# Splitting the last chunk of a graph attention kernel into two softmax units of four groups, with older groups added up two per slot

## What is computed

```python
f = (x @ W_ni.T)[src] + (x @ W_nj.T)[dst] + e @ W_fij.T
f = leaky_relu(f, 0.2)
score = f @ attn
a = softmax of score over the edges of each dst
h = x @ W_node.T
h_out = segment_sum(h[src] * a[:, None], dst)
```

## Time and profile before

| | |
|---|---|
| median of 3 runs | 2160.43 us (2159.26 to 2163.89) |
| the profiled execution's own time | 2163.74 us |
| its span | 2162.0 us |
| mean granted TensorE clock | 0.92 |
| busy share PE, POOL, DVE, ACT | 87%, 74%, 63%, 31% |

### The profile page before, as it was taken

One profiled execution on the slowest core, in us unless ns is written; L12 is line 12 of the kernel. 1 busy time (PEld: TensorE's weight loads), 2 busy tenths in 40 slices (PEclk: granted clock), 3 DMA queues, 4 the chain that ended last, 5 costly groups with the idle time before them and its releaser, 6 DMA issues.

```text
span 2162.0 us, 41030 instructions
## 1 busy us (share of the span) xinstructions
PE 1872.9 (87%) x10816; PEld 1284.3 (59%) x10816; DVE 1351.5 (63%) x4574; ACT 672.6 (31%) x1260; POOL 1593.5 (74%) x1664
## 2 busy tenths in 40 slices
PE   5799999898888899898978998888888888888887
PEld 4366766566565666566756666565555555565656
DVE  6477776665665666665745756656556556555655
ACT  2555444443433434443211112222222222122221
POOL 7777777777777777777577777777777777777771
PEclk9899999989999989988989989989999999989998
DMA  9888898888888888888756776666766766766761
GB/s 321 261 269 287 281 290 268 255 259 253 262 256 254 262 247 266 261 252 252 228 163 181 216 203 199 207 198 195 207 191 201 204 197 197 205 190 199 204 195 41
DMA packets 352481, 490.63 MB, mean 227 GB/s; under 512 B 115219, under 2 KB 217924, under 8 KB 352092
## 3 DMA queue, kind: packets, MB, share of 16 engines
q1 hardware_dynamic: 236803, 249.78, 38.0%
q0 software_dynamic: 78416, 212.69, 33.4%
q10 hardware_dynamic: 37017, 25.40, 3.9%
HBM read 409.00 MB, written 81.38 MB: 227 GB/s over the span
## 4 chain that ended last, share of the span: by engine, by line
PE 41%; DMA 23%; issue 12%; POOL 9%; DVE 7%; ACTq 6%; ACT 2%; POOLq 0%; DVEq 0%; SPq 0%
DMA xsrc<-h_table,idx_slot 11%; PE bSC L935 9%; DMA xsrc<-x_table,idx_slot 9%; POOL xsrc L612 9%; PE pair L946 9%; PE pair L894 8%; PE pair L915 7%; ACTq L778 4%; PE pair L919 3%; ACTq L774 2%; DVE fT L1419 1%; DMA proj<-xsrc 1%; ACT zc L738 1%; PE bX L1000 1%; DVE amat L1267 1%
## 5 line engine op out<-in xcount | busy, mean ns | idle before, releaser
L612 POOL DMA_INDIRECT xsrc<-h_table,idx_slot x804 | 777.1, 967 | 246.9 <-issue 201.3
L612 POOL DMA_INDIRECT xsrc<-x_table,idx_slot x767 | 730.8, 953 | 233.8 <-issue 194.2
L738 ACT ACTIVATE zc<-pair 128x512 f32<-128x512 f32 x416 | 248.4, 597 | 1334.4 <-PE pair L919 1137.7
L1419 DVE TENSOR_TENSOR fT<-pair,zc 128x512 f32<-128x512 f32 x416 | 286.1, 688 | 350.9 <-ACT zc L738 348.1
L894 PE MATMUL pair<-edge_in,wts 128*128 128x512 f32 x832 | 488.3, 670 | 10.3 <-DMA window<-proj 10.3
L915 PEld LDWEIGHTS pair<-ident,xsrc 128*128 128x128 f32 x1600 | 204.8, 152 | 472.1 <-DMA xsrc<-h_table,idx_slot 213.6
L935 PE MATMUL bSC<-fT,attn_at 128*32 128x128 f32 x3328 | 478.9, 291 | 3.7 <-DVE fT L1419 3.7
L946 PEld LDWEIGHTS pair<-amat,xsrc 128*128 128x128 f32 x3328 | 432.8, 201 | 64.1 <-issue 50.6
L946 PE MATMUL pair<-amat,xsrc 128*128 128x42 f32 x3328 | 465.2, 293 | 2.2 <-DVE amat L1269 2.0
L915 PE MATMUL pair<-ident,xsrc 128*128 128x128 f32 x1600 | 275.1, 299 | 191.7 <-DMA xsrc<-h_table,idx_slot 119.5
L935 PEld LDWEIGHTS bSC<-fT,attn_at 128*32 128x32 f32 x3328 | 350.2, 116 | 113.9 <-issue 92.0
(11 more groups left out here) (169 smaller groups left out, 1407.5 us busy)
## 6 DMA issues: line engine op xcount, KB each, us to landing
edge_in<-eT SPq DMA_DIRECT2D x208, 256.0 KB
rel_bc<-relrow_g SPq DMA_DIRECT2D x416, 128.0 KB
h1T<-h SPq DMA_DIRECT2D x208, 256.0 KB
edge_in<-h1T SPq DMA_DIRECT2D x208, 256.0 KB
stage<-h_table ACTq DMA_DIRECT2D x896, 1.0 KB
window<-proj SPq DMA_DIRECT2D x416, 32.0 KB
xsrc<-h_table,idx_slot POOLq DMA_INDIRECT x824, 3.7
xsrc<-x_table,idx_slot POOLq DMA_INDIRECT x767
```

What stands on the lines that cost most here:

```text
L612: pool.indirect_dma_start(xsrc[b][:, i, 0:width], None, table, bass.IndirectOffsetOnAxis(ap=idx_slot[b][:, i:i + 1], axis=0)).then_inc(L.g ...
L738: nc.scalar.mul(zc[s][:, :], bZ[s][:, :], SLOPE).then_inc(L.z_scaled, 1)
L1419: v.tensor_tensor(fT[s][:, :], bZ[s][:, :], zc[s][:, :], ALU.max).then_inc(L.f_made, 1)
```

## The change

The last chunk becomes two units: unit 25 is groups 200 to 203, unit 26 is groups 204 to 207 (16 rows of scores each). Unit 25's softmax steps lie in slots 204 to 208, unit 26's in slots 208 to 212. Slot 208 still adds up group 195; slots 209 to 212 add up two groups each (196 and 197, ..., 202 and 203), and slots 213 to 216 one each (204 to 207). The program ends in slot 217. Slab 24 is summed in slot 212. `dst_rows` is loaded twice in the last chunk, at its slots 2 and 6, behind the `row_maxima` of units 24 and 25; `masks` run in its slots 3 and 7. `FILL` has fewer idle matmuls. Unit 25 has its own weight tiles (`relc_next`, `wcol_next`). Cut to its core:

```diff
-FILL = {0: 1, 1: 2, 2: 5, 3: 3, 4: 2, 5: 1}
+FILL = {0: 1, 1: 1, 2: 2, 3: 1, 4: 2, 5: 1}
+HALF = 4
+def soft_steps(c, g):
+    if not isinstance(c, int):
+        return {g: c - 1} if g <= 4 else {}
+    slot = c * GC + g
+    return {slot - closed(u): u for u in range(CH + 1) if 0 <= slot - closed(u) <= 4}
+def summed(c, g):
+    if not isinstance(c, int):
+        return [c * GC + (g - LAG)]
+    slot = c * GC + g
+    if slot <= NG:
+        return [slot - LAG] if slot >= LAG else []
+    first = NG - LAG + 2 * (slot - NG) - 1
+    if first < NG - HALF:
+        return [first, first + 1]
+    n = slot - (LAG - HALF)
+    return [n] if n < NG else []
...
-                        if g == GC - 2:
-                            if isinstance(c, int) and c == 0:
+                        if g == GC - 2 or (isinstance(c, int) and c == CH - 1 and g == GC - HALF - 2):
+                            u = CH if isinstance(c, int) and c == CH - 1 and g == GC - 2 else c
+                            if isinstance(u, int) and u == 0:
...
-                                sp.wait_ge(L.soft_dve, (c - 1) * 6 + 1)
+                                sp.wait_ge(L.soft_dve, (u - 1) * 6 + 1)
...
+                        for m in sums[1:]:
+                            partial(m // GC, m % GC, m // GC % XB)
...
+                        if static:
+                            past, coming = summed(c, g - 1), summed(c, g + 1)
+                            for m in past[0:1]:
+                                finish(m)
+                            for m in coming[0:1]:
+                                weighted_onehot(m, m % GC, True)
...
+                        if static and c == CH - 1:
+                            if g == GC - HALF - 1:
+                                masks(CH - 1)
+                            if g == GC - 1:
+                                masks(CH)
+                        elif front and g == 6:
                             masks(c)
+                        if static:
+                            for m in past[1:]:
+                                finish(m)
+                            for m in coming[1:]:
+                                weighted_onehot(m, m % GC, True)
```

More of the change, by code:

```diff
@@ L143, in slab_at, with unit_of, first_group, closed @@
     return k * (2 * NB) - LEAD, NB
+def unit_of(n):
+    return CH if n >= NG - HALF else n // GC
+def first_group(u):
+    return NG - HALF if isinstance(u, int) and u == CH else u * GC
+def closed(u):
+    return NG - HALF if isinstance(u, int) and u == CH - 1 else NG if isinstance(u, int) and u == CH else u * GC + GC
+def height(u):
+    return HALF * TG if isinstance(u, int) and u >= CH - 1 else TC
+def soft_steps(c, g):
[14 more added lines that the diff above has]
+    return [n] if n < NG else []
+def slab_steps(n, c, g):
+    if isinstance(c, int):
+        slot = c * GC + g
+        late = (CH + 1) * GC
+        if n == 2 and late - GC <= slot <= late - GC + 4:
+            steps = {late - GC + i: {name: CH - 3} for i, name in enumerate(("rest", "std", "shift", "out", "store"))}
+            steps[late - GC + 4].update(sum=CH - 2, h=CH - 2)
+            return steps[slot]
+        if slot >= late - GC + 4:
+            names = {late - 4: ("sum", "h"), late - 3: ("rows",), late - 2: ("copies", "rest") if n == 1 else ("rest",),
+                     late - 1: ("middle", "low") if n == 1 else ("std", "shift"),
+                     late: ("store",) if n == 1 else ("out", "store")}.get(slot, ())
+            return {name: CH - 2 for name in names}
+    plan = {}
+    if not (isinstance(c, int) and not 2 <= c <= CH - 1):
+        plan.update({6: {"sum": c - 2, "h": c - 2}, 7: {"rows": c - 2}}.get(g, {}))
+    if not (isinstance(c, int) and c < 3):
+        at = ({0: ("copies", "rest"), 1: ("middle", "low"), 2: ("store",)} if n == 1 else
+              {0: ("rest",), 3: ("std",), 4: ("shift",), 5: ("out",), 6: ("store",)})
+        plan.update({name: c - 3 for name in at.get(g, ())})
+    return plan
 def above(eng, sem, value):
@@ L740, in slot @@
                         one_hot(c, g + 1)
[L741 to L747, removed]
[L748 to L753 removed]
+                    steps = soft_steps(c, g)
+                    if 0 in steps:
+                        u, rows = steps[0], height(steps[0])
+                        act.wait_ge(L.score_made, closed(u))
+                        above(act, L.soft_dve, u * 6 - 3)
+                        nc.scalar.copy(score_sb[0:rows, :], bSC[0:rows, 0:P]).then_inc(L.score_copied, 1)
+                    if 2 in steps:
+                        u, rows = steps[2], height(steps[2])
+                        act.wait_ge(L.soft_dve, u * 6 + 3)
+                        nc.scalar.activation(aexp[0:rows, :], seg[0:rows, :], ACT.Exp)
+                        nc.scalar.activation(ecar[0:1, 1:2], ecar[0:1, 0:1], ACT.Exp).then_inc(L.soft_act, 1)
+                    if narrow:
+                        plan = slab_steps(L.n, c, g)
+                        for name, body in (("copies", slab_copies), ("middle", slab_middle), ("std", slab_std),
+                                           ("out", slab_out), ("store", slab_store)):
+                            if name in plan:
+                                body(L, plan[name])
                     if L.n == 1 and isinstance(c, int) and n < 2 * GC - 1:
@@ L1242, in normalise @@
+                    step(v.scalar_tensor_tensor(seg[rows, :], isL[rows, :], cd[rows, 1:2], seg[rows, :],
+                                                ALU.mult, ALU.add))
                     step(v.reciprocal(cfac[0:1, 0:1], seg[0:1, 0:1]))
```

266 lines of the change are left out of this document (153 added, 113 removed).

## The result

The changed kernel takes 2217.57 us (median of 4 runs, 2216.62 to 2218.79), the kernel before on the same chip 2161.98: ratio 1.0257, 95% interval 1.0242 to 1.0271, so 55.6 us slower. The profiled execution has a span of 2215.7 us, 53.7 more than before, and the same mean granted clock, 0.92.

A forecast was written before the change was run, and what follows sets the result against it. Bounds: each layer's softmax chain and additions, and slab stores ahead of layer 2's gathers. Layer 1's 22.4 us, layer 2's 10.7 and 5 for the clock made 38.1: 2202 profiled, 2199 on the median; range 2174 to 2218.

The forecast's parts named there:

- A: Last chunk, z(201) to z(207): loads held behind `dst_rows` delay z, 11 us in layer 1, 3.2 in layer 2.
- B: From z(207) to the end of unit 26's `row_maxima`: unit 25's softmax end goes first, plus 3.2 us each layer.
- C: From unit 26's `row_maxima` to its `weight_cols`: two groups a slot add one-hots and waits, 7.6 us each layer.
- slow and cold case: Rival: 7.7 us for each load and half clock throughout, 51.9 us slower, 2212; chance 0.10.
- D: After unit 26's `weight_cols`: fewer groups save 3.3 us in layer 2; slab 24's store costs 0.6 in layer 1.
- E: Slots 208 to 213: fewer idle matmuls and TensorE's waits may halve its clock, 0 or 9.8 us, 5 taken.
- first hold: Layer 1, last chunk's slot 2: group 202's load waits for unit 24's `row_maxima`; z(202) 3.7 us later, 3.5 stays.
- The hold is hidden: Rival: loads land sooner or gathers alone set the pace, so held loads cost about 0; 2184.3, chance 0.12.

The follow-up runs named there:

- e9_covered: e8_three_no_fills with 20 idle matmuls where TensorE waits for unit 25's softmax and through the last softmax; 2172.6 us against 2166.5 for the kernel before, ratio 1.0027.
- e5_early_reads: The changed kernel with the 12 register reads of turn 26 made three at a time in slots 203 to 206; 1.0147 of the kernel before.
- e4_one_a_slot: The changed kernel with its two softmax units but one older group per slot, as before; 1.0117 of the kernel before.
- e8_three_no_fills: e6_three_mended without the eight idle matmuls of the last softmax; 2775.8 us, 1.0051 of the kernel before.
- c2_before: The kernel before, unaltered, profiled on a slower chip; 2766.1 us.
- e6_three_mended: The changed kernel with own destination-row tiles for units 25 and 26, a third buffer and early register reads together; 1.0069 of the kernel before.
- e3_old_fills: The changed kernel with the last softmax's idle matmuls put back to 14 from 8; 1.0193 of the kernel before.

## Why the prediction was right, and where its sizes were off

The direction and the mechanisms of A, B and C were right: each of these stretches is longer, by the wait or the work named, and slower was shown with an interval far from 1. But 38.1 us were forecast and 55.6 came. 2217.57 lies 0.4 us inside the range, beyond even the slow and cold case (2212): that it lies inside is luck. Two sizes were far off, the saving of D did not come, and the cause given for E was wrong. The terms:

- **A, right in kind, 14.2 forecast, 12.9 measured.** In layer 1 the loads took 5.4 and 4.5 us, not 6, 2.1 us of the first hold stayed where I let 3.5 stay, and 8.1 came instead of 11. The 3.0 us that the prediction worked out for such a load from the Trainium skill (DMA: Bandwidth & Descriptors, "Anatomy of one DMA") rest on a fit to transfers that GpSimd issues; these are SyncE's, and took 4.5 to 5.4. In layer 2 the load cost more than I said (4.8 for 3.2). That the one-hots wait for the held loads is shown: in no run with tiles of their own do they wait. What the hold costs on the first chip is argued from the rows above and from e9_covered, where A falls by 4.5 and 5.7 us; an edit of A alone was not run on such a chip. "The hold is hidden" does not fit the first chip, and is open on the three slower ones, where the waits went and A hardly changed.
- **B, 6.4 forecast, 12.4 measured.** The term left out the register read, 2.73 us in each layer; e5_early_reads shows 2.4 to 2.7 of it. The failed step is "`masks` add 1.2, `weight_cols` 0.75": between them stands the turn's first instruction, which the trace of before had too, covered by a wait. With it the sum would have been 5.9 a layer, against 6.7 and 5.7. The 0.8 left in layer 1 is VectorE's own work: the 3.7 us up to `normalise` were read in layer 2, where there is no `h1` (0.68) and `row_sums` end sooner.
- **C and E, 15.2 and 5 forecast, 26.8 measured in C alone.** Where the waits stand was right, to the one-hot. Their size was not: I put a partial at its full-clock time and half of the clock's price beside it as a separate, even chance. The waits are the partial itself, so the clock multiplies them: 2.16 for 1.2. Step E's "none or all: 0 or 9.8; I take half" is the step that failed. The Trainium skill (TensorE: Matmul & The Clock Gate, "HAM oscillation — how this bites in real kernels") says that waits between groups of matmuls can send the clock back to half, and the trace agrees: 0.50 through C in both layers. The clock alone does not do it: with one group a slot C is 12.3 and 11.8 us at half clock (e4_one_a_slot). In the runs C's 13 us a layer fall apart like this: 5.0 to 7.6 waits between the engines, 4.5 to 4.9 idle matmuls at half clock that no longer stand in idle time, and 2.2 to 4.5 for VectorE's four more one-hots and the softmax's own steps at half clock (e8_three_no_fills against c2_before; I said 3.3). The three add up to 1.5 too much, by which C is longer in e6_three_mended than with the third buffer alone; that remainder is not explained.
- **D, -2.7 forecast, +4.2 measured.** The saving of fewer groups behind `weight_cols` did not come: the adds of layer 2 take 15.5 us at 0.50. They take 13.9 with a third buffer, 11.0 without idle matmuls as well (e8_three_no_fills, still at 0.50) and 8.3 at 1.00 in e9_covered, so of the 7.2 us between, about 2.7 are the clock. In layer 1 the prediction's terms up to the store's landing (2.8, 1.9, 1.3, 0.7 and 4.0) make 10.7, not 10.2, so its 0.6 should have read 1.1; 3.5 came.
- **The cause of E** was named as fewer idle matmuls. That is refuted: putting them back makes it worse (e3_old_fills). TensorE has too little work in B, where unit 25's softmax keeps VectorE, and in this kernel the clock that is at half at the start of C stays there (e9_covered, with idle matmuls from slot 207 on, keeps it).
- **Not forecast:** 3.9 us come back at the start of layer 2, where VectorE is no longer late for the first gathers.

The missed 2.73 us had a rule. The Trainium skill (Runtime: NRT & Kernel Launch, "Instruction fetch mechanics") gives about 200 ns for each register of a `TENSOR_LOAD`, which is what the trace calls L1408; 12 values would be 2.4 us, an estimate from that page. The rows here, reads from SBUF, agree nearly: 2.73 for 12 values, 1.85 for eight, mostly 0.74 to 0.76 for three (1.09 in the row above).

The experiments lead from 1.0257 to 1.0027 but to nothing that beats the kernel before. With the waits, reads and clock mended VectorE is busy in 11.8 us of layer 2's C, against 8.9 before, and C is 4.0 us longer than before where B is 3.0 longer and the adds 6.5 shorter.

## What to carry to other kernels

When work is doubled up in a slot, look at its buffers: two things that were settled a slot earlier become a wait for the partner's whole operation, and a third buffer is part of the change. Put a clock that may fall into the duration of every serial step, not beside the sum, and look for its cause in the idle time ahead of the stretch. Idle matmuls that stood only behind it cost 3.1 to 3.6 us a layer here; with some ahead of it too the clock was kept, but in layer 2's C they cost more than it brought. An instruction that a wait hides, here a register read, is priced as soon as the change fills that wait. When you count rows of a trace to find the n-th event, check first that all of them are there.

## What the runs showed of the hardware

- A TensorE that starts a stretch at 1.2 GHz can stay there while the trace shows it busy nearly all the time: 18.40 of 18.40 us in e6_three_mended and 13.28 of 13.48 in e8_three_no_fills at 0.50.
- The kernel before ran 2162 and 2166 us on two chips and 2766 to 2802 on three others, its granted clock 0.92 on the first and 0.80 on the one of c2_before; its B and C were the same on these two to within 1 us.
- Reading values from SBUF into VectorE's registers holds its queue for 0.52 us for one value, 0.74 to 0.76 mostly for three, 1.85 for eight and 2.73 for 12.
